# Layer 0 of a graph network: weights and node numbers in PSUM, the destination one-hot on ScalarE, two small products on VectorE

## The reference

```python
xl = (x @ W_l).reshape(N, HEADS, C)
xr = (x @ W_r).reshape(N, HEADS, C)
h = xl[src] + xr[dst]
e = jnp.einsum('ehc,hc->eh', jax.nn.leaky_relu(h, NEG_SLOPE), att)
emax = jax.ops.segment_max(e, dst, num_segments=N)
p = jnp.exp(e - emax[dst])
denom = jax.ops.segment_sum(p, dst, num_segments=N)
alpha = p / denom[dst]
msg = alpha[:, :, None] * xl[src]
out = jax.ops.segment_sum(msg, dst, num_segments=N).reshape(N, HID) + bias
```

## Time and profile before

| | us |
|---|---|
| median of three runs | 4747.33 (4744.81 to 4748.25) |
| the profiled execution | 4730.89 |
| its span in the profile | 4729.0 |
| first stage, node tables | about 0 to 140 |
| edge sweep of layer 0 | about 140 to 2240 |
| layer 1 and the ends | from 2240 |

### The profile page before, as it was taken

The page is one execution under the profiler, slowest core; times in us unless marked ns, Lnnn a source line. Parts: engine busy times, 40 slices in busy tenths (PEclk is TensorE's granted clock), DMA queues, the critical chain, the costliest instruction groups (busy, mean ns, idle before and its releaser), DMA issues. The chain is left out here.

```text
span 4729.0 us, 71029 instructions
## 1 busy us (share of the span) xinstructions
PE 3216.0 (68%) x16994; PEld 2342.8 (50%) x16995; DVE 2549.1 (54%) x7518; ACT 592.0 (13%) x1636; POOL 3300.4 (70%) x3295
## 2 busy tenths in 40 slices
PE   6899999999999999999593433343333434433448
PEld 4555555565555655555483333343333333333337
DVE  7577677667666666766483333333333333333337
ACT  3111111111111111111260000000000000000006
POOL 3777777777777777776246777777777777777750
PEclk9899999999999999999796667766766676677669
DMA  6544444444444444443443333333333333333323
GB/s 183 164 111 112 112 113 112 112 112 113 113 112 113 112 112 113 112 113 99 110 114 99 103 99 95 104 100 99 104 96 102 99 100 99 99 104 99 98 71 100
DMA packets 463435, 512.49 MB, mean 108 GB/s; under 512 B 183038, under 2 KB 363134, under 8 KB 463398
## 3 DMA queue, kind: packets, MB, share of 16 engines
q1 hardware_dynamic: 280646, 262.38, 19.2%
q0 software_dynamic: 100352, 208.93, 18.0%
q10 hardware_dynamic: 82400, 40.77, 3.0%
HBM read 464.45 MB, written 47.30 MB: 108 GB/s over the span
## 5 line engine op out<-in xcount | busy, mean ns | idle before, releaser
L469 POOL DMA_INDIRECT rows<-xl_table,src_idx x1568 | 1587.9, 1013 | 533.6 <-issue 513.2
L469 POOL DMA_INDIRECT rows<-x_table,src_idx x1568 | 1598.6, 1020 | 489.4 <-issue 476.8
L1075 PE MATMUL pT<-relu_h,node_of 128*128 128x128 f32 x1584 | 367.8, 426 | 1017.8 <-DVE node_of L1109 1017.8
L1075 PEld LDWEIGHTS pT<-relu_h,node_of 128*128 128x128 f32 x1584 | 341.2, 327 | 1039.0 <-DVE node_of L1109 1039.0
L535 PE MATMUL ph<-node_of,xr_win 128*128 128x512 f32 x784 | 752.7, 1094 | 1.3 <-issue 1.3
L1075 PE MATMUL pA<-relu_h,edge_of 128*128 128x128 f32 x3136 | 483.7, 319 | 259.7 <-DVE relu_h L1125 259.7
L1075 PEld LDWEIGHTS pA<-relu_h,edge_of 128*128 128x128 f32 x3136 | 461.9, 234 | 278.9 <-DVE relu_h L1125 278.9
L1125 DVE TENSOR_TENSOR relu_h<-rows,dst_row 128x1024 f32<-128x1024 f32 x196 | 241.0, 1229 | 566.0 <-DMA rows<-x_table,src_idx 566.0
L572 PE MATMUL pA<-wmsg,edge_of 128*128 128x136 f32 x3168 | 425.7, 288 | 6.8 <-DVE edge_of L789 6.3
L561 PE MATMUL pT<-att_heads,relu_h 128*128 128x56 f32 x3136 | 391.3, 278 | 1.3 <-DVE shifted L818 1.3
L572 PEld LDWEIGHTS pA<-wmsg,edge_of 128*128 128x128 f32 x3168 | 385.6, 192 | 11.4 <-issue 8.0
(11 more groups left out here) (154 smaller groups left out, 3637.6 us busy)
## 6 DMA issues: line engine op xcount, KB each, us to landing
dst_row<-in_dst SPq DMA_DIRECT2D x196, 513.0 KB
dst_row<-in_edge_attr SPq DMA_DIRECT2D x195, 512.0 KB
rows<-xl_table,src_idx POOLq DMA_INDIRECT x1568
rows<-x_table,src_idx POOLq DMA_INDIRECT x1568
sums_table<-win ACTq DMA_DIRECT2D x198, 68.0 KB
rows<-in_x SPq DMA_DIRECT2D x100, 128.0 KB, 2.4
xr_win<-xr_table SPq DMA_DIRECT2D x196, 64.0 KB
sums_table<-win ACTq DMA_DIRECT2D x1, 6868.0 KB
```

Source lines behind the costliest of these rows:

```text
L469: pool.indirect_dma_start(rows[s][:, t, 0:table.shape[1]], None, table[:, :], bass.IndirectOffsetOnAxis(ap=src_idx[s][:, t:t + 1], axis=0))\
L1075: ins = pe.matmul(banks[k][:, 0:D], edge_buf[k][:, t, :], m[:, t, :], start=(t == 0), stop=(t == T - 1))
```

## The change

Five things change in the sweep of layer 0.

1. node_of is made by ACT in two operations, the absolute distance to the first node and the relu of one less that distance. DVE only makes first_node.
2. The exponentials are written a second time, to the tensor weights in the PSUM bank pT1, and weigh reads them from there. The node numbers near_row are copied once to the same bank, and edge_one_hot reads them from there.
3. The product L563 goes. DVE adds the linear part to the products in front of the scans, into logits in SBUF.
4. The product L586 goes. DVE adds carried to the first message of the group, in one partition.
5. weigh is split: what concerns carried is now the function carry and keeps its place. weigh itself moves from the step of g + 1, behind the scans, to the end of the step of g, behind prepare.

The core of the diff:

```diff
+        products, logit = logit_all[:, 0:H * T], logits[:, :]
+        weights = pT1[:, 2 * P:2 * P + H * T].rearrange("p (h t) -> p h t", h=H)
+        near_row = pT1[:, 3 * P:4 * P]
...
-                    linear = rows[g.c % U][:, :, D:DW].rearrange("p t h -> p h t")
-                    pe.matmul(by_head(logit), ident[:, :], linear, start=False, stop=True).then_inc(S("logit_ready"), 1)
+                    ins.then_inc(S("products_ready"), 1)
...
-                    visit(0)
-                    pe.matmul(pA[0][:, 0:WC], first_row[0:1, :], carried[0:1, :], start=False, stop=True)\
-                      .then_inc(S("summed"), 1)
+                    visit(0).then_inc(S("summed"), 1)
...
+                def node_one_hot(g):
+
+                    s, of = g.c % U, node_of[g.c % 2][:, :]
+                    act.wait_ge(S(f"row_in0{s}"), g.use(16, 16))
+                    act.wait_ge(S("first_made"), g.times(1, 1))
+                    if g.at_least(2):
+                        act.wait_ge(S("h_ready"), g.times(2, -2))
+                    act.activation(of, dst_row[s][:, 1:1 + G], ACT.Abs, scale=-1.0, bias=first_node[:, s:s + 1])\
+                       .then_inc(S("distance_made"), 1)
+                    act.wait_ge(S("distance_made"), g.times(1, 1))
+                    act.activation(of, of, ACT.Relu, scale=-1.0, bias=one[:, :]).then_inc(S("node_of_made"), 1)
...
                         act.wait_ge(S("shifted_ready"), g.times(1, 1))
                         heads = wmsg[g.c % 2][:, :, 0:H * HC].rearrange("p t (h k) -> p t h k", k=HC)
+                        act.activation(weights, shifted[:, :, 0:T], ACT.Exp)
...
+                    if not (g.j is None and g.c + 2 >= groups):
+                        node_one_hot(g + 2)
...
-                    hide.at(g.times(HIDE_LINKS))
-                    hide.link(v.tensor_tensor(first, node_id[:, 0:1], dst_row[s][:, 1:2], ALU.add))
-                    if g.at_least(2):
-                        v.wait_ge(S("h_ready"), g.times(2, -2))
-                    v.tensor_scalar(node_of[g.c % 2][:, :], ids, first, None, ALU.is_equal)\
-                     .then_inc(S("node_of_made"), 1)
+                    v.tensor_tensor(first_node[:, s:s + 1], node_id[:, 0:1], dst_row[s][:, 1:2], ALU.add)\
+                     .then_inc(S("first_made"), 1)
...
-                    v.wait_ge(S("logit_ready"), g.times(1, 1))
+                    v.wait_ge(S("products_ready"), g.times(1, 1))
+                    linear = rows[g.c % U][:, :, D:DW].rearrange("p t h -> p h t")
+                    soft.link(v.tensor_tensor(by_head(logit), by_head(products), linear, ALU.add))
...
-                                    heads[:, :, :, C:HC].to_broadcast([P, T, H, C]), ALU.mult)\
+                                    weights.rearrange("p h t -> p t h").unsqueeze(3).to_broadcast([P, T, H, C]), ALU.mult)\
                      .then_inc(S(f"rows_free0{s}"), 1)
+
+                def carry(g):
+
                     if g.at_least(1):
...
-                                        ALU.mult)
+                                        ALU.mult).then_inc(S("carried_made"), 1)
+                        v.wait_ge(S("carried_made"), g.times(1, 1))
+                        v.tensor_tensor(first_message, first_message, carried[:, 0:H * HC], ALU.add)
...
-                                                        node_row[:, :].unsqueeze(1).to_broadcast([P, T, P]), ALU.is_equal)
+                                                        near_row.unsqueeze(1).to_broadcast([P, T, P]), ALU.is_equal)
...
                     if g.at_least(1):
-                        weigh(last)
+                        carry(last)
...
                     if not (g.j is None and g.c + 1 >= groups):
                         prepare(g + 1)
+                    if more:
+                        weigh(g)
```

More of the change, by code:

```diff
@@ L41 @@
 GAT_SLOPE, MLP_SLOPE, EPS = 0.2, 0.01, 1e-5
-SOFT_LINKS = 8
+SOFT_LINKS = 9
 PREPARE_LINKS = 3
-HIDE_LINKS = 1
 class Group:
@@ L179, in build @@
         b1 = sb("b1", [P, 1])
+        one = sb("one", [P, 1])
         eps = sb("eps", [P, 1])
@@ L204, in build @@
         dst_big, dst_rel = sb("dst_big", [P, T + 2]), sb("dst_rel", [P, T])
-        fwd, run = sb("fwd", [P, H * T]), sb("run", [P, H * T])
+        logits, fwd, run = (sb(n, [P, H * T]) for n in ("logits", "fwd", "run"))
         step_pen = sb("step_pen", [P, H * T + 1])
@@ L394, in _ @@
                 v.memset(eps[:, :], EPS)
+                v.memset(one[:, :], 1.0)
                 v.memset(step_pen[:, :], -BIG)
@@ L560, in attend @@
                             pe.wait_ge(S("relu_ready"), g.times(2, 1 + t // 4))
-                        pe.matmul(out_t[:, t, :], relu_h[0][:, t, :], att_heads[:, :], start=(t == 0), stop=False)
-                    linear = rows[g.c % U][:, :, D:DW].rearrange("p t h -> p h t")
-                    pe.matmul(by_head(logit), ident[:, :], linear, start=False, stop=True).then_inc(S("logit_ready"), 1)
+                        ins = pe.matmul(out_t[:, t, :], relu_h[0][:, t, :], att_heads[:, :], start=(t == 0), stop=(t == T - 1))
+                    ins.then_inc(S("products_ready"), 1)
                 def sum_up(g, span):
@@ L572, in visit @@
                             ins = pe.matmul(pA[k][:, 0:WC], edge_of[k][:, t, :], w[:, t, :],
-                                            start=(t == 0), stop=(t == T - 1 and k == 1))
+                                            start=(t == 0), stop=(t == T - 1))
                         return ins
@@ L669, in keep @@
                     further_windows(act, n, span, further)
+                def node_one_hot(g):
[8 more added lines that the diff above has]
+                    act.activation(of, of, ACT.Relu, scale=-1.0, bias=one[:, :]).then_inc(S("node_of_made"), 1)
                 def step(g, near):
                     if not g.at_least(1):
+                        node_one_hot(g)
+                        node_one_hot(g + 1)
                         relu(g)
@@ L697, in _, with first_of @@
                 v.sem_inc(S("dst_taken0"), U)
-                soft, hide = Chain(v, S("soft_chain")), Chain(v, S("hide_chain"))
-                def node_one_hot(g):
+                soft = Chain(v, S("soft_chain"))
+                v.tensor_copy(near_row, node_row[:, :]).then_inc(S("near_row_made"), 1)
+                v.wait_ge(S("near_row_made"), 1)
+                def first_of(g):
                     s = g.c % U
-                    first, ids = first_node[:, s:s + 1], dst_row[s][:, 1:1 + G]
                     v.wait_ge(S(f"row_in0{s}"), g.use(16, 16))
-                    hide.at(g.times(HIDE_LINKS))
-                    hide.link(v.tensor_tensor(first, node_id[:, 0:1], dst_row[s][:, 1:2], ALU.add))
-                    if g.at_least(2):
-                        v.wait_ge(S("h_ready"), g.times(2, -2))
-                    v.tensor_scalar(node_of[g.c % 2][:, :], ids, first, None, ALU.is_equal)\
-                     .then_inc(S("node_of_made"), 1)
+                    v.tensor_tensor(first_node[:, s:s + 1], node_id[:, 0:1], dst_row[s][:, 1:2], ALU.add)\
+                     .then_inc(S("first_made"), 1)
                 def further_one_hots(g, span):
@@ L826, in step @@
                     if not g.at_least(1):
-                        node_one_hot(g)
+                        first_of(g)
+                        first_of(g + 1)
                         further_one_hots(g, near(g))
-                        node_one_hot(g + 1)
                         prepare(g)
@@ L843, in step @@
                     if not (g.j is None and g.c + 2 >= groups):
-                        node_one_hot(g + 2)
+                        first_of(g + 2)
                     if not (g.j is None and g.c + 1 >= groups):
                         prepare(g + 1)
+                    if more:
+                        weigh(g)
                 sweep(v, groups, step, spans)
```

2 lines of the change are left out of this document (1 added, 1 removed).

## The result

The changed kernel takes 4892.68 us (median of 4, from 4875.08 to 4913.45) against 4747.79 us before: a ratio of 1.0305, with a 95% interval of 1.0283 to 1.0328. It is 145 us slower, where 220 had been forecast. The profiled execution took 4875.08 us with a span of 4873.3.

What follows compares the result with a forecast made beforehand. PE and the short chain ending each step were taken as the bound, POOL only just keeping up. 11.04 + 0.10 + 0.16 + 0.64 = 11.94 us a step against 10.81, 220 us more, about 4968 us; range 4790 to 5070.

Steps and rivals of the forecast that it cites:

- rival (a): Layer 0's sweep: same chain, but the clock dips no more often than today; step 11.45 us, total 4872; chance 0.19.
- The chain: Each step: scans and L611 queue behind the weighing, which waits for ACT's exponentials behind copy L657; 11.04 us a step.
- Rival (b): DVE's gap: weighing fits in if ACT's exponentials come ahead of L657; 60 us less, 4687; chance 0.09.
- The loop's end: DVE's register load, now behind the weighing, costs 0.4 us more every fourth step, 0.10 a step.
- The clock: PE after longer pauses: 0.16 us a step for slower work, 0.64 for dips to 1.2 GHz in 80% of steps.
- Rival (d): PE: two clock dips a step, slowing the sums or L561 too; 156 us more, 5123; chance 0.06.
- The ACT one-hot: ACT behind the exponentials: two operations, about 1.03 us each, end about 0.1 after the following L611, beside other work.
- Operands in PSUM: DVE's weighing and edge one-hot read one operand from PSUM at 0 cost, at most 0.05 us each.
- The two products: PE: dropping L586 saves 0.43 us, L563 nothing; about 0.39 a step together, 76 us, if PE sets the pace.
- Rival (c): POOL is the true bound and gathers faster with L709 gone and PSUM reads; 156 us less, 4591; chance 0.05.

Runs made afterwards that it cites:

- e5: The kernel before with only the weighing moved to the end of the step, ahead of the next group's scans: 4888.1 us, ratio 1.0350.
- e4: The changed kernel with ACT's exponentials of group g put ahead of keep of group g - 1: 4636.39 us, ratio 0.9819 to the kernel before.
- e3: The changed kernel with five more unused 128 by 128 products on PE in its pause: 4795.31 us, ratio 1.0147 to the kernel before.
- e1: The changed kernel with the weighing put back behind the scans, reading from SBUF: 4771.57 us, ratio 1.0099 to the kernel before.
- e8: e1 with ACT's one-hot of g + 2 at the start of step g and first_of behind the scans: 4694.75 us, ratio 0.9939.
- e12: e6 with the node numbers for the edge one-hot in PSUM: 4677.63 us, ratio 0.9900 to the kernel before.
- e6: The kernel before with only the two small products replaced by additions on DVE: 4738.65 us, ratio 1.0028.
- e2: The changed kernel with the weighing in its new place but reading from SBUF, without the third exponential: 4845.37 us, ratio 1.0266 to the kernel before.

## Why the prediction was right

The mechanism was right; the size was 0.72 a step and not 1.13. The measured 4893 us lies 21 above rival (a), at 4872, and 75 below the forecast of 4968.

**The chain.** The step that decides, scans queued behind weighing and exponentials, was right, and each of its terms behind the sums is within 0.06 of the trace. e5 shows the place as a cause by itself, and e4 shows which link is at fault: the order of keep and the exponentials on ACT. Rival (b) had named that as its condition, with a step of 10.5 on the mean; e4 measured 10.37.

**The loop's end.** The pause before L611 there is 2.10 instead of 1.75 on the mean, so 0.35 more every fourth step; 0.4 was taken.

**The clock** is the term that was mis-sized. The forecast had 0.64 for dips in 80% of the steps and 0.16 for slower work behind a pause, 0.80 together. Slow transpositions came in 51% of the steps, and e3, which takes away both, gives 0.39 for both. The price of one was nearly right: a step with them is 0.74 longer, 11.90 against 11.16, and 0.51 x 0.74 = 0.38. The share was too high, and the 0.16 hardly exists: without slow transpositions the sums end 7.27 after L611, where the same steps of the kernel before have 7.23. With 0.39 in place of 0.80 the sum is 11.04 + 0.10 + 0.39 = 11.53, the step that was measured. That it fits to 0.01 is partly luck, as 7.27 and the chain behind the sums, 3.88 with the loop's end where 3.95 was summed, err to opposite sides. What sets the share stays open. It is not the length of the pause alone: 59% behind pauses of 1.06 before, 51% with 1.84, and 13 of 190 steps in e4, whose mean pause is 1.01. Rival (d) had the sums slow as well; from 400 to 1400 us none of them ran at the lower clock.

**The ACT one-hot** "lies beside other work": true in the changed kernel. It ends 0.20 after L611 in the step shown, where 0.1 was forecast; that DVE's wait goes on for 0.49 behind it was not foreseen. The two operations take 1.133 and 1.148, not 1.03, which is what the line from the earlier trace rows gave. The Trainium skill (ScalarE: Activation LUTs, What ACT_TABLE_LOAD costs) has a formula that gave 1.13, and the trace agrees. Once the weighing is back the one-hot does cost time: the step of e1 is 11.07, and that of e8, which has it early, 10.66, where POOL stops it.

**Operands in PSUM** at nothing: right for DVE, whose weighing takes 1.221 against 1.220. By the fixed costs that the Trainium skill gives (VectorE: DVE Perf Modes, The TRN2 errata) it should have grown by 65 ns, an estimate; the trace does not agree, and the measurement decides. It was wrong to look at DVE alone. The operand's place matters for POOL, where it is worth 1.3% in e12.

**The two products** at 76 us "if PE went on setting the pace": it did not. e6 shows POOL as the second bound that takes the gain. The waits had shown PE to be the first bound; how near the second was stood in the earlier trace rows, where POOL waited just 10.7 us in 2000. All its gaps beyond 0.30 add up to 52 us, so POOL could have gone at about 10.5 a step before; e6 lengthened its gathers from 1.014 to 1.056, and that makes the 10.9. Rival (c) was wrong on the kernel before, and right on what would be late next. Relieving POOL alone in the kernel before was not run; its edge one-hot had little to give, as the gathers that start under it last 0.94 already.

## What to carry to other kernels

Before a step is moved ahead on an in-order engine, ask what its wait depends on and who is queued behind it; here the wait reached back through another engine's order to the same step's matrix products, and exchanging two blocks on that engine turned 3% of loss into 2% of gain. Where two engines are both nearly full, work taken off one brings nothing until the other is relieved as well, and a releaser line of almost no waiting is the sign. A pause of TensorE can cost more than its length, by the clock; useless products in it were worth 1.5%.

## What had not been expected of the hardware

A wide DVE operation with both operands in SBUF makes a gather that starts under it last up to 1.7 to 2.0 us instead of 0.94, and one operand in PSUM brings that back to 0.94. In four kernels with the weighing from SBUF, the gathers that start under it last 1.44 to 1.53 on the mean (e1, e2, e6, e8). It depends on how much of the operation is still to run when the gather starts. In e1, over 200 to 2100 us:

| of the weighing still to run, us | gathers | mean length, us |
|---|---|---|
| under 0.2 | 8 | 0.95 |
| 0.2 to 0.4 | 8 | 1.13 |
| 0.4 to 0.6 | 38 | 1.35 |
| 0.6 to 0.8 | 53 | 1.49 |
| 0.8 to 1.0 | 31 | 1.72 |
| 1.0 to 1.2 | 34 | 1.90 |
| over 1.2 | 4 | 0.94 |

So a gather is held for about as long as the operation goes on, and one that starts together with it is not held. In the kernel before, the edge one-hot had both operands in SBUF too, and 115 gathers start under it in that stretch; but 95 of them start in its last 0.03 us and 20 in its first 0.02, and all last 0.94 to 0.95. In e5, where the same one-hot is met earlier, the gathers under it last 1.55.
